# Moving the first product of the row maxima from the score stage into the value stage, one batch earlier

## The reference

```python
scores = jnp.einsum('bhsr,bhlr->bhsl', q_r, k_r)      # 16 heads x 56 queries, 1500 keys of 64 numbers
attn = jax.nn.softmax(scores, axis=-1)
ctx_c = jnp.einsum('bhsl,bld->bhsd', attn, kv_rope)   # 1500 values of 64 numbers
```

## Time and profile before

| what | value |
|---|---|
| time, median of 3 runs | 2128.64 us (2125.79 to 2129.28) |
| the profiled execution's own time | 2128.17 us |
| its span in the trace | 2126.4 us |
| PE busy | 2040.6 us (96%) |
| DVE busy | 1485.2 us (70%) |
| POOL busy | 1359.4 us (64%) |
| ACT busy | 1074.6 us (51%) |
| mean granted TensorE clock | 0.994 of full speed |

### The profile page before, as it was taken

One profiled execution on the slowest core, in us unless ns is written; L12 is line 12 of the kernel. 1 busy time (PEld: TensorE's weight loads), 2 busy tenths in 40 slices (PEclk: granted clock), 3 DMA queues, 4 the chain that ended last, 5 costly groups with the idle time before them and its releaser, 6 DMA issues.

```text
span 2126.4 us, 35215 instructions
## 1 busy us (share of the span) xinstructions
PE 2040.6 (96%) x13564; PEld 1422.9 (67%) x13568; DVE 1485.2 (70%) x2141; ACT 1074.6 (51%) x1770; POOL 1359.4 (64%) x850
## 2 busy tenths in 40 slices
PE   7998999999999998999999999999999999999998
PEld 5787777765565556766555655588897655655588
DVE  6869871588888857666788888653335888888653
ACT  4552332565665656211665665544434656656543
POOL 0368873188788785454788788634441887887644
PEclk9999999999999999999999999999999999999999
DMA  3035776423223104102223222025533232231022
GB/s 99 11 119 178 248 240 202 96 59 88 59 59 88 45 31 140 26 1 63 59 64 83 59 64 68 22 79 156 149 91 78 59 88 59 59 88 45 33 54 72
DMA packets 65704, 179.59 MB, mean 84 GB/s; under 512 B 11280, under 2 KB 21280, under 8 KB 65154
## 3 DMA queue, kind: packets, MB, share of 16 engines
q1 hardware_dynamic: 65154, 177.01, 31.5%
q10 hardware_dynamic: 384, 0.33, 0.1%
HBM read 162.32 MB, written 14.98 MB: 83 GB/s over the span
## 4 chain that ended last, share of the span: by engine, by line
PE 80%; DVE 7%; ACT 5%; POOL 3%; issue 3%; DMA 1%; POOLq 0%; DVEq 0%; SPq 0%; ACTq 0%
PE psum L962 20%; PE psum L1551 19%; PE psum L1537 18%; PE psum L1425 5%; PE psum L1436 3%; ACT E L2011 3%; PE psum L976 3%; PE psum L1709 3%; PE psum L1568 2%; PE psum L1666 2%; PE psum L1354 1%; POOL CL L2030 1%; PE psum L1252 1%; PE psum L1232 1%; DVE ST L2826 1%
## 5 line engine op out<-in xcount | busy, mean ns | idle before, releaser
L2563 DVE TENSOR_REDUCE mx<-psum 128x2 f32<-128x1000 f32 (+1 forms) x540 | 552.5, 1066 | 164.2 <-PE psum L1425 161.7
L2292 POOL TENSOR_TENSOR SA<-SA,E 125x896 f32<-125x896 f32 x288 | 606.3, 2105 | 19.0
L2011 ACT ACTIVATE E<-psum 125x896 f32<-125x896 f32 x576 | 512.7, 918 | 101.2 <-PE psum L1537 83.2
L1551 PE MATMUL psum<-E,V 125*64 125x448 f32 x2304 | 449.4, 539 | 0.0
L1551 PEld LDWEIGHTS psum<-E,V 125*64 125x64 f32 x2304 | 163.4, 137 | 246.4 <-issue 239.0
L1537 PE MATMUL psum<-QH,KH 64*125 64x448 f32 x1152 | 255.3, 399 | 10.2 <-ACT E L2011 4.2
L1537 PE MATMUL psum<-QL,KH 64*125 64x448 f32 x1152 | 241.4, 365 | 0.0
L2292 POOL TENSOR_TENSOR SA<-E,E 125x896 f32<-125x896 f32 x48 | 101.5, 2115 | 200.3 <-PE psum L1425 152.1
L1537 PE MATMUL psum<-QH,KL 64*125 64x448 f32 x1152 | 228.1, 363 | 0.0
L1425 PE MATMUL psum<-KH,QH 64*128 64x500 f32 x864 | 182.0, 405 | 1.8 <-ACT QR L1953 1.6
L2585 DVE RECIPROCAL RS<-psum 128x448 f32<-128x448 f32 x48 | 142.0, 2957 | 46.0 <-PE psum L1568 45.5
(11 more groups left out here) (310 smaller groups left out, 4302.1 us busy)
## 6 DMA issues: line engine op xcount, KB each, us to landing
KH<-kt_scratch SPq DMA_DIRECT2D x96, 375.0 KB, 5.3
KL<-kt_scratch SPq DMA_DIRECT2D x96, 375.0 KB, 7.1
EW<-in_f_w SPq DMA_DIRECT2D x64, 256.0 KB, 5.9
kt_scratch<-kt SPq DMA_DIRECT2D x16, 750.0 KB, 6.4
WS<-in_f_w SPq DMA_DIRECT2D x31, 384.0 KB, 4.7
GB<-gates_scratch SPq DMA_DIRECT2D x36, 224.0 KB, 3.8
slot_of_t<-slots_scratch SPq DMA_DIRECT2D x64, 112.0 KB, 4.4
WoT<-in_a_WoT SPq DMA_DIRECT2D x24, 256.0 KB, 3.4
```

Of the source, the lines that this page charges most:

```text
L1551: i = e.matmul(psum[c * DC:(c + 1) * DC, 4, 0:HT], V[0:LP, b, tile * DC:(tile + 1) * DC], E[g[n, b, k] % NE][0:LP, half[c]], start=k == 0, ...
L2011: e.activation(E[m % NE][0:LP, :].rearrange("p (c q) -> p c q", c=2), psum[0:LP, pair:pair + 2, 0:HT], ACT.Exp).then_inc(exp_set.sem, 1)
L2292: e.tensor_tensor(SA[b % 2][0:LP, :], a[0:LP, :], x[0:LP, :], ALU.add).then_inc(sum_set.sem, 1)
L2563: e.tensor_reduce(o, psum[:, max_banks(kind, *t), 0:CW], AX.X, ALU.max).then_inc(small_free.sem, 1)
```

## The change

The pair (0, 0) of the maxima of a batch is issued one stage earlier. For batch 1 it stays at k = 0 of the score stage of batch 0. For batches 2 to 15 it is issued behind `values` k = 7 of the batch two before, instead of ahead of `head` k = 0 of the batch one before. DVE's reduction of it moves with it, since DVE reads the same list.

```diff
@@ core_order
         for k in range(NL):
-            order += [("max", b + 1, *MAX_AT[k])] if following and k in MAX_AT else []
+            order += [("max", b + 1, *MAX_AT[k])] if following and k in MAX_AT and (k > 0 or b == 0) else []
             order.append(("head", b, k))
...
             if k == 4 and following:
                 order.append(("max_spread", b + 1))
+            if k == 7 and b + 2 < B:
+                order.append(("max", b + 2, 0, 0))
             if k == 8:
                 order += [("div", b - 1)] if b > 0 else []
```

## The result

The changed kernel takes 2142.26 us (median of 3 runs, 2141.65 to 2145.08) against 2128.64 us before: ratio 1.0077, 95% interval 1.0059 to 1.0095. It is slower, by 13.6 us at the medians (a ratio of 1.0064); the interval of the ratio is 12.6 to 20.2 us. Forecast were 2143.0 us and +14.3 us.

What follows compares the result with a forecast made beforehand. PE was taken to set the pace. 42 x (0.57 - 0.23) = +14.3 us on the profiled 2128.2 us gave 2142.5 us, and 0.5 us for the median 2143.0 us; range for 8 in 10: 2129 to 2153 us.

Steps and rivals of the forecast that it cites:

- The price: Value stage on PE: the moved pair costs 0.57 us there, against 0.23 us among products of its own kind.
- three parts: From the last product of `values` 7 to the second of `values` 8: 0.47 + 0.42 + 0.43 = 1.32 us, before 0.75 us.
- the return: PE going back from the pair's row halves to the values' column halves: 0.42 us from pair to next product.
- The gain: Score stage without the pair at its head: second product, first exponential and all later waits 0.23 us earlier.
- the slack of 0.24 us: Score stage: the eviction ends 0.66 us in, the pair (1, 0) that needs it is issued 0.9 us in.
- What was hidden: Value stage: the pair's inputs and banks are ready, and its reduction ahead of `div` delays nothing needed.
- The slack of `div`: Value stage on DVE: `div` ends at 600.87, the eviction waiting for it comes at 602.30, 1.4 us left.
- The sum: All three layers: 42 x (0.57 - 0.23) = +14.3 us, giving 2143.0 us, 0.67% slower.
- Mode changes free: Rival, value stage: the pair costs 0.23 us in both places, the move nothing: 2128.6 us; chance 0.12.
- No gain in the score stage: Rival: the score stage does not get its 0.23 us back: +24 us, 2152.6 us; chance 0.09.
- DVE the bound: Rival, score stage: DVE's chain gets shorter by a whole reduction: -23 us, 2105.5 us; chance 0.09, wholly or in part.
- `div` late: Rival, value stage: the reduction in front of `div` holds up the eviction: +35 us, 2164 us; chance 0.03.

Runs made afterwards that it cites:

- experiment 2: Kernel before, with one extra row-half pair of maxima on PE alone, no reduction, behind `values` 7: 2153.53 us, ratio 1.0116.
- Experiment 3: Kernel before, with an extra float32 pair in the values' column halves behind `values` 7, same waits and bank: 2136.35 us, ratio 1.0039.
- Experiment 4: Changed kernel, with the moved pair issued twice in a row on PE, one reduction: 2154.78 us, ratio 1.0124 to the kernel before.
- experiment 1: Kernel before, with the pair (0, 0) of batches 2 to 15 left out, product and reduction: 2115.77 us, ratio 0.9939.
- Experiment 6: Changed kernel, with the pair behind `values` 8 and behind `div` in the list: 2142.72 us, ratio 1.0077 to the kernel before.
- experiment 10: Kernel before, with the first five pairs of maxima one tile later (k = 1 to 5): 2144.34 us, ratio 1.0080.

## Why the prediction was right

**The price, 0.57 us per pair.** Right: 0.567 us by experiment 2, and each of its three parts (0.85 - 0.38 = 0.47, 0.42 and 0.43 us) stands in the trace after. That the return was read from a pair among 128 x 128 products, and from an end product ahead of the total, did no harm. That the cause is the change between row and column halves was an argument at the time. Experiment 3 and the two sets of rows beside it show it: the price falls to 0.205 us when mode and number type are kept, a change of division costs 0.4 us without a change of type, and a change of type costs nothing without a change of division. The Trainium skill ("TensorEngine Tiling (Array Packing)", Key Properties) says that a change of tiling mode drains TensorE; experiments 2 to 4 agree that such a change costs time and give its size here, 0.567 - 0.229 = 0.34 us for the two changes of one visit. That this time is spent on a drain, and not on something else in the change, no run shows.

**The gain, 0.23 us per score stage.** Right: 0.229 us by experiment 1. All later waits of the stage did move with it. The pair (1, 0) was issued 0.91 us into the stage and the eviction that it needs ended at 0.66 us, so the slack of 0.24 us was as forecast.

**What was hidden.** Right in effect. The slack of `div` was sized at 1.4 us and is 0.9 us, since `div` itself took 1.15 us, not 0.61 us: the working did not ask what POOL does at that time (below). Experiment 6 shows that it costs nothing.

**The sum.** For 14 visits in each of three layers, 42 x (0.567 - 0.229) = 14.2 us; forecast 14.3 us, measured 13.6 us at the medians. That these two agree to 0.7 us is partly luck, since the three times of the changed kernel alone span 3.4 us and the profiled execution differs from the one before by 16.9 us. What bears the sum out is the period: 23.08 us from eviction to eviction against a forecast of 23.10 us.

**The rivals.** Mode changes free: refuted by experiments 2 and 3. No gain in the score stage: refuted by experiment 1. DVE the bound: refuted by experiment 1, while experiment 10 shows how near it was. `div` late: refuted by experiment 6. No order was found that is faster than the kernel before; that the maxima could be had more cheaply in some other way stays open.

## What to carry to other kernels

A product moved "into idle time" of other engines is priced by its neighbours on TensorE: here a pair cost its columns (0.23 us) among products of its own tiling and 0.57 us among products of another, so count the changes of mode per period before and after. An engine that is busy for 12.3 us of a 12.6 us stage need not be its bound: look for the first gap in its run, which here was also its margin. If a kernel repeats a period, read the distance between two far marks in the trace; here it resolved 0.01 us per period, where run times resolve a few microseconds in all.

## What the runs showed of the hardware that was not expected

`div` on DVE reads two operands from SBUF, and POOL's addition of SB to SA, which reads SBUF too, runs at the same time. Which comes first decides who is longer. The rows of each, by tile, in layer 1's batches (minimum, median and maximum in ns), for the kernel before:

```profile
L2590 DVE TENSOR_TENSOR QR<-OB,RS x14: 612/615/653, 462.0 to 757.9; 128x448 f32<-128x448 f32 x14
...
L2292 POOL TENSOR_TENSOR SA<-SA,SB x15: 2085/2333/2355, 439.9 to 758.1; 125x896 f32<-125x896 f32 x15
```

after the change:

```profile
L2592 DVE TENSOR_TENSOR QR<-OB,RS x14: 617/1152/1223, 467.3 to 765.9; 128x448 f32<-128x448 f32 x14
...
L2294 POOL TENSOR_TENSOR SA<-SA,SB x15: 2082/2089/2337, 443.2 to 766.1; 125x896 f32<-125x896 f32 x15
```

and in experiment 6:

```profile
L2591 DVE TENSOR_TENSOR QR<-OB,RS x14: 612/612/722, 465.7 to 765.9; 128x448 f32<-128x448 f32 x14
...
L2293 POOL TENSOR_TENSOR SA<-SA,SB x15: 2087/2337/2352, 443.2 to 766.1; 125x896 f32<-125x896 f32 x15
```

With `div` first, it takes 0.61 us and POOL 2.33 us; with POOL first, POOL takes 2.09 us and `div` 1.15 us. Only the later one is longer.

In the changed kernel a reduction stands in front of `div` as well, and experiment 6 takes both away at once. Experiment 4 separates them: the reduction is still in front, but the two stand 0.23 us later against POOL's addition. These are POOL's addition after the change, in the batch whose `div` starts at 605.81 us, and then POOL's addition and `div` in experiment 4, with `div` over all batches of layer 1 as the last row:

```profile
604.39 2.09 POOL L2294 TENSOR_TENSOR SA<-SA,SB 125x896 f32<-125x896 f32 x1 [0.29 <-DVE SB L2583]
```

```profile
603.96 2.08 POOL L2295 TENSOR_TENSOR SA<-SA,SB 125x896 f32<-125x896 f32 x1 [0.38 <-DVE SB L2584]
605.61 0.93 DVE L2593 TENSOR_TENSOR QR<-OB,RS 128x448 f32<-128x448 f32 x1
L2593 DVE TENSOR_TENSOR QR<-OB,RS x14: 615/930/971, 465.6 to 767.0; 128x448 f32<-128x448 f32 x14
```

`div` is shorter by 0.22 us, nearly what it starts later. It ends 0.48 us behind POOL's end after the change (606.96 and 606.48) and 0.50 us behind it in experiment 4 (606.54 and 606.04). So it is POOL that `div` waits for, not the reduction. The Trainium skill ("SBUF — State Buffer", section SBUF: two separate sides) states that a DVE instruction with two SBUF inputs and a GpSimd instruction that reads SBUF take turns at a shared pair of ports, whole instruction by whole instruction, the first to start first. The trace agrees to 0.13 us: by that rule `div`, 0.61 us long alone, would end 0.61 us behind POOL. Both had cover here, so it cost no time.
